# A graph layer on one core: the joined result turned by 32x32 blocks on VectorE, with stores and loads of 128-byte runs

## The chip, the cores and the metric

One Trainium2 chip, one of its cores. The metric is the device time of one execution in microseconds (us). Engines are named as in the profile: PE is TensorE (PEld its weight loads), DVE is VectorE, ACT is ScalarE, POOL is GpSimd, SP is SyncE; SPq is SP's own queue, from which the transfers are issued.

## The reference, cut to what matters

```python
# x (16, 512, 128), adj (16, 512, 512), W (7, 144, 128), W_edges (7, 16), b (512, 128), all float32
h = maximum(layernorm(x), 0)
A = [adj, adj, shifted, adj.T, adj.T, shifted.T, eye]          # seven relations
HW[r] = h @ W[r, :128] + (W_edges[r] @ W[r, 128:])              # a constant row per relation
out = x + max over r of (A[r] @ HW[r]) + b
```

`shifted` is a rolled identity. The kernel treats relations 2, 5 and 6 (its `EYE`) without an adjacency, 0 and 1 (`FWD`) with adj, 3 and 4 (`BWD`) with its transpose. The kernel forms adj @ h and adj.T @ h once each and multiplies them by W afterwards.

## The kernel before, in words

Sixteen batches are worked one after the other, two to a turn of the loop (`k` is the pair, `q` the half, b = 2k + q); nearly all tiles are doubled (`x_sb`, `a_sb`, `best`, `o_sb` ..., one for each q). Every engine has its own hand-written order of work, and semaphores tie them together. I call "step b" what `step(k, q, left)` (L297, L412, L580, L816) issues.

Everything is computed feature by node: a 128x512 tile has the features on the partitions and the 512 nodes of a batch along the row. Every float32 product is made of three passes (L720) over high and low parts (`a_hi`/`a_lo`, `h_hi`/`h_lo` and so on).

In step b TensorE does, in this order: `fwd` of the batch (four chunks of three passes), between them the relations of `EYE` and the two `FWD` relations of the batch before (`along`, L774); then it turns the first half of the next batch's adjacency (`turn_a`, L678) and its h (`turn_h`, L692); then `bwd` with the `BWD` relations of the batch before; then the second half of the next adjacency; and last `turn_best` (L712): four transposes of 128x128, which bring the finished maximum of the batch before (`best`, feature by node) to node by feature in the PSUM bank `turn_ps`.

VectorE keeps the running maximum (`join`, L534) and makes low parts; at the start of step b its `finish` (L545) adds the turned maximum from `turn_ps` and `xb_sb` (x plus bias) into `o_sb`. ScalarE makes the high parts, and `fill` (L381) writes row sums of the adjacency, times a constant, into the PSUM banks in which `along` then adds. GpSimd makes the low parts of the adjacency (`split_a`, L264) and of h (`split_h`, L271), the reciprocal deviation, and `xb_sb` (`add_bias`, L279), which reads the same `x_sb` as the layer norm.

SP issues every transfer. In step b (L211): store of batch b-2 when `out_ready` says so (L209, one transfer, runs of 512 bytes); x of batch b+2 (L177), which waits for `h_ready` and `xb_ready`; the adjacency of batch b+2 (L180) in four transfers of 256 KB, each when its piece of `a_lo` is made; then `spread_sums` (L196): the row sums (8x128) go to DRAM (L201), SP waits for them to be stored (L202), and one transfer copies them to all 128 partitions (`sum_all`, L203, 512 KB written). In step 0 `spread_sums` stands first. All these transfers stand in one queue and use the same 16 DMA engines.

After step 15 there is a tail: the last relations, the last `turn_best(k, 0)` (batch 14), and for batch 15 two halves of 256 columns: join (L666), transposes (L880), add (L673) and two stores on SP (L246).

Of the kernel before, what the change touches and what calls it, by code (L numbers as in the profile page):

```python
# [6 lines left out]
def gnn_layer(nc, x, adj, W, W_edges, bias, out):  # L7

# [25 lines left out]
    S = 2 * C  # L34
    PAIRS = B // 2
# [3 lines left out]
    with ctx:  # L39
# [22 lines left out]
        bias_sb = sb("bias_sb", [P, C, O])  # L62
# [8 lines left out]
        xb_sb = pair(sb, "xb_sb", [P, C, F])  # L71
# [21 lines left out]
        o_sb = pair(sb, "o_sb", [P, C, O])  # L93
# [9 lines left out]
        def at_bank(b, i):  # L103
# [6 lines left out]
        x_loaded = pair(sem, "x_loaded")  # L110
# [29 lines left out]
        half_filled, half_done, half_joined, half_turned, half_out_ready = (  # L140
            sem(s) for s in ("half_filled", "half_done", "half_joined", "half_turned", "half_out_ready"))
# [29 lines left out]

        block = ctx.enter_context(nc.Block())

        @block.sync
        def _(sp):
            def load_x(k, q):
                sp.dma_start(x_sb[q][:], x[2 * k + q, :, :].rearrange("(j p) f -> p j f", p=P)).then_inc(x_loaded[q], 16)  # L177

            def load_a(k, q, j):
                sp.dma_start(a_sb[q][:, j, :], adj[2 * k + q, j * P:(j + 1) * P, :]).then_inc(a_loaded[q][j], 16)  # L180

            def reload_x(k, q):

                b = 2 * k + q
                sp.wait_ge(h_ready, b + 1)
                sp.wait_ge(xb_ready, b + 1)
                load_x(k + 1, q)

            def reload_a(k, q):
                b = 2 * k + q  # L190
                sp.wait_ge(a_turned[C - 1], b + 1)
                for j in range(C):
                    sp.wait_ge(a_lo_ready[j], b + 1)
                    load_a(k + 1, q, j)

            def spread_sums(k, q):  # L196
# [4 lines left out]
                sp.dma_start(sums_dram[q][:, :], sum_rows[q][:]).then_inc(sums_stored[q], 16)  # L201
                sp.wait_ge(sums_stored[q], 16 * (k + 1))  # L202
# [4 lines left out]
            def store(k, q):  # L207
                sp.wait_ge(out_ready, 2 * k + q + 1)
                sp.dma_start(out[2 * k + q, :, :].rearrange("(j p) o -> p j o", p=P), o_sb[q][:]).then_inc(out_stored[q], 16)  # L209

            def step(k, q, more, stored=True):  # L211

                if isinstance(k, int) and k == 0 and q == 0:
                    spread_sums(k, q)
                if stored:
                    store(k - 1, q)
# [3 lines left out]
                if not (isinstance(k, int) and k == 0 and q == 0):  # L220
# [14 lines left out]
            sp.dma_start(bias_sb[:], bias.rearrange("(j p) o -> p j o", p=P)).then_inc(bias_loaded, 16)  # L235
# [8 lines left out]
            for half, (ready, count) in enumerate(((half_out_ready, 1), (out_ready, B))):  # L244
                sp.wait_ge(ready, count)
                sp.dma_start(out[B - 1, half * HALF:(half + 1) * HALF, :].rearrange("(j p) o -> p j o", p=P),  # L246
                             o_sb[1][:, half * C // 2:(half + 1) * C // 2, :]).then_inc(out_stored[1], 16)
            sp.wait_ge(out_stored[0], 16 * PAIRS)
            sp.wait_ge(out_stored[1], 16 * (PAIRS + 1))

        @block.gpsimd
        def _(pool):
# [26 lines left out]
            def add_bias(k, q):  # L279
                b = 2 * k + q  # L280
                pool.wait_ge(x_loaded[q], 16 * (k + 1))
                wait(pool, out_ready, b - 1)
                pool.tensor_tensor(xb_sb[q][:], x_sb[q][:], bias_sb[:], ALU.add).then_inc(xb_ready, 1)  # L283

            def first_step():
# [7 lines left out]
                pool.wait_ge(bias_loaded, 16)  # L293
                add_bias(0, 0)
                add_bias(*ahead)

            def step(k, q, left):  # L297
                if is_batch(2 * k + q, 1):
# [4 lines left out]
                    split_a(k, q, 3)  # L303
                else:
# [22 lines left out]
            later_batches(pool, step)  # L327

        @block.scalar
        def _(act):  # L330
            def round_a(k, q, j):
                b = 2 * k + q
                act.wait_ge(a_loaded[q][j], 16 * (k + 1))
# [154 lines left out]
            fill(k, q, BWD[1], bwd_ps, filled[BWD[1]], slice(HALF, N))  # L488

        @block.vector  # L490
        def _(dve):
# [53 lines left out]
            def finish(k, q):  # L545
# [357 lines left out]
```

## Time and profile before

| what | us |
|---|---|
| device time of three executions | 229.6, 229.86, 560.38 |
| their median | 229.86 |
| the profiled execution's own device time | 230.07 |
| span of its trace | 228.3 |

The trace begins 0 us at its first instruction; what lies outside the span is 230.07 - 228.3 = 1.8 us. The granted TensorE clock is 0.998 of full over the run.

### The profile page before, as it was taken

How to read it: one execution, taken by the hardware profiler on the slowest of the kernel's cores; microseconds unless marked ns; L12 is line 12 of the kernel's file. 1: busy time of each engine (PE TensorE's matmuls, PEld its weight loads, DVE VectorE, ACT ScalarE, POOL GpSimd, SP SyncE). 2: the span in 40 equal slices, each digit the busy share in tenths (PEclk: the TensorE clock that was granted, in tenths of full speed). 3: DMA queues.
4: the chain of work that ended last, by engine and by line, in shares of the span. 5: the costliest groups of instructions: out<-in, count | busy, mean ns of one | idle time of the engine just before them, and what ended most of it. 6: DMA issues, size and time to landing. Idle time of an engine off the chain costs nothing.

```text
span 228.3 us, 4799 instructions
## 1 busy us (share of the span) xinstructions
PE 217.5 (95%) x1133; PEld 179.8 (79%) x1133; DVE 177.7 (78%) x387; ACT 186.1 (82%) x468; POOL 143.0 (63%) x163
## 2 busy tenths in 40 slices
PE   7888999999999999999999999999999999999981
PEld 5567677888888888888888888888888888888761
DVE  4896798787978878787878878787887879767473
ACT  3868998888988888897988889798888889886640
POOL 2491679578493948758493966949395784937200
PEclk9999999999999999999999999999999999999999
DMA  5948454726436372744537372653547265121203
GB/s 186 295 120 277 135 140 138 229 97 199 172 117 190 107 230 92 226 143 140 188 97 224 115 228 114 167 191 91 198 135 222 101 162 207 49 81 60 92 0 95
DMA packets 30385, 34.52 MB, mean 151 GB/s; under 512 B 2103, under 2 KB 20135, under 8 KB 30375
## 3 DMA queue, kind: packets, MB, share of 16 engines
q1 hardware_dynamic: 30375, 34.41, 47.4%
q8 instruction: 4, 0.07, 0.1%
q14 instruction: 6, 0.05, 0.1%
HBM read 30.14 MB, written 4.26 MB: 151 GB/s over the span
## 4 chain that ended last, share of the span: by engine, by line
PE 86%; DVE 5%; issue 2%; ACT 2%; DMA 2%; SPq 0%; DVEq 0%; ACTq 0%
PE at_ps L689 11%; PE rel_ps L721 11%; PE rel_ps L723 11%; PE rel_ps L722 11%; PE fwd_ps L721 6%; PE bwd_ps L721 6%; PE bwd_ps L723 6%; PE bwd_ps L722 6%; PE fwd_ps L723 6%; PE fwd_ps L722 6%; PE turn_ps L701 3%; PE turn_ps L717 3%; DMA a_sb<-in_adj 2%; DVE h_lo L635 1%; DVE best L540 1%
## 5 line engine op out<-in xcount | busy, mean ns | idle before, releaser
L268 POOL TENSOR_TENSOR a_lo<-a_sb,a_hi 128x512 fp32r<-128x512 f32 x62 | 79.2, 1301 | 53.5 <-ACT a_hi L336 53.5
L543 DVE TENSOR_TENSOR best<-rel_ps,best 128x512 f32<-128x512 f32 x62 | 42.4, 683 | 17.2 <-PE rel_ps L723 16.5
L514 DVE TENSOR_TENSOR at_lo<-at_ps,at_hi 128x512 fp32r<-128x512 f32 x62 | 41.1, 683 | 6.8 <-ACT at_hi L344 6.7
L384 ACT ACTIVATE rel_ps<-sum_all,c_col 128x512 f32<-128x512 f32 (+1 forms) x63 | 41.8, 679 | 3.8 <-DVE best L543 3.1
L336 ACT ACTIVATE a_hi<-a_sb 128x512 fp32r<-128x512 f32 x64 | 39.4, 616 | 3.5 <-DMA a_sb<-in_adj 3.5
L344 ACT ACTIVATE at_hi<-at_ps 128x512 fp32r<-128x512 f32 x62 | 36.3, 590 | 7.1 <-PE at_ps L689 7.1
L689 PEld LDWEIGHTS at_ps<-ident,a_sb 128*128 128x128 f32 x240 | 28.1, 141 | 4.1
L689 PE MATMUL at_ps<-ident,a_sb 128*128 128x128 f32 x240 | 31.2, 272 | 0.0
L540 DVE SCALAR_TENSOR_TENSOR best<-rel_ps,c_col,best 128x512 f32<-128x512 f32 x32 | 24.0, 750 | 5.7 <-PE rel_ps L723 4.5
L721 PE MATMUL fwd_ps<-at_hi,h_hi 128*128 128x512 f32 x64 | 26.8, 419 | 1.2 <-DVE at_lo L514 1.0
L721 PE MATMUL bwd_ps<-a_hi,h_hi 128*128 128x512 f32 x64 | 26.6, 415 | 0.3 <-POOL a_lo L268 0.3
L723 PE MATMUL fwd_ps<-at_hi,h_lo 128*128 128x512 f32 x64 | 25.2, 394 | 0.0
L723 PE MATMUL bwd_ps<-a_hi,h_lo 128*128 128x512 f32 x64 | 25.2, 393 | 0.0
L722 PE MATMUL fwd_ps<-at_lo,h_hi 128*128 128x512 f32 x64 | 25.0, 391 | 0.0
L722 PE MATMUL bwd_ps<-a_lo,h_hi 128*128 128x512 f32 x64 | 25.0, 390 | 0.0
L354 ACT ACTIVATE h_sb<-x_sb,shift,rstd 128x128 f32<-128x128 f32 x60 | 24.6, 483 | 0.0
L276 POOL TENSOR_TENSOR h_lo<-h_sb,h_hi 128x512 fp32r<-128x512 f32 x14 | 17.9, 1279 | 6.6 <-DVE h_hi L508 6.6
L283 POOL TENSOR_TENSOR xb_sb<-x_sb,bias_sb 128x512 f32<-128x512 f32 x16 | 21.0, 1318 | 1.4 <-DVE o_sb L550 1.4
L392 ACT ACTIVATE best<-rel_ps,c_col 128x512 f32<-128x512 f32 x16 | 11.0, 689 | 12.3 <-PE rel_ps L723 12.3
L721 PE MATMUL rel_ps<-ht_hi,w_hi 128*128 128x512 f32 x48 | 19.3, 401 | 1.4 <-issue 0.9
L722 PE MATMUL rel_ps<-ht_lo,w_hi 128*128 128x512 f32 x48 | 19.0, 395 | 0.0
L723 PE MATMUL rel_ps<-ht_hi,w_lo 128*128 128x512 f32 x48 | 18.9, 393 | 0.0
(104 smaller groups left out, 437.2 us busy)
## 6 DMA issues: line engine op xcount, KB each, us to landing
a_sb<-in_adj SPq DMA_DIRECT2D x64, 256.0 KB, 4.1
sum_all<-sums_dram SPq DMA_DIRECT2D x16, 512.0 KB, 3.6
x_sb<-in_x SPq DMA_DIRECT2D x16, 256.0 KB, 2.9
out<-o_sb SPq DMA_DIRECT2D x15, 256.0 KB, 2.3
w_sb<-in_L_gnn_W SPq DMA_DIRECT2D x1, 448.0 KB, 5.6
bias_sb<-in_L_gnn_b SPq DMA_DIRECT2D x1, 256.0 KB, 4.8
sums_dram<-sum_rows SPq DMA_DIRECT2D x16, 4.0 KB
out<-o_sb SPq DMA_DIRECT2D x2, 128.0 KB, 2.5
```

The lines of the kernel that those rows point to most:

```text
L268: pool.tensor_tensor(a_lo[q][:, j, :], a_sb[q][:, j, :], a_hi[q][:, j, :].bitcast(fp32), ALU.subtract).then_inc(a_lo_ready[j], 1)
L336: act.activation(a_hi[q][:, j, :], a_sb[q][:, j, :], ACT.Copy, accum_out=sums[q][:, 0, j:j + 1]).then_inc(a_hi_ready[j], 1)
L344: act.activation(at_hi[q][:, i, :], at_bank(b, i)[:], ACT.Copy, accum_out=sums[q][:, 1, i:i + 1]).then_inc(at_hi_ready[i], 1)
L354: last = act.activation(h_sb[q][:, j, :], x_sb[q][:, j, :], ACT.Relu, bias=shift[q][:, j:j + 1], scale=rstd[q][:, j:j + 1])
L384: act.activation(to[:, cols], sum_all[q][:, 0 if r in FWD else 1, cols], ACT.Copy, scale=c_col[:, r:r + 1]).then_inc(after_it, 1)
L514: dve.tensor_tensor(at_lo[q][:, i, :], at_bank(b, i)[:], at_hi[q][:, i, :].bitcast(fp32), ALU.subtract).then_inc(at_lo_ready[i], 1)
L540: dve.scalar_tensor_tensor(out=best[q][:], in0=held[:], scalar=c_col[:, r:r + 1], in1=best[q][:], op0=ALU.add, op1=ALU.max).then_inc(joine ...
L543: dve.tensor_tensor(best[q][:], held[:], best[q][:], ALU.max).then_inc(joined[r], 1)
L689: last = pe.transpose(at_bank(b, i)[:, j * P:(j + 1) * P], a_sb[q][:, j, i * P:(i + 1) * P], ident[:])
L721: pe.matmul(out, w_hi_, m_hi, start=start, stop=False, skip_group_check=onto)
L722: pe.matmul(out, w_hi_, m_lo, start=False, stop=False, skip_group_check=onto)
L723: return pe.matmul(out, w_lo_, m_hi, start=False, stop=stop, skip_group_check=onto)
```

## The change

- The turned result no longer passes through TensorE and `turn_ps`. VectorE turns `best` by blocks of 32x32 (`dve.transpose`, at the end of its step, after `split_fwd`) into a new tile pair `turned`. In it partition 32g + n, column 32c + f holds feature 32g + f of node 32c + n.
- GpSimd, not VectorE, adds `turned` and `xb_sb` into `o_sb` (`finish`), after the second `split_a` pair of its step; `add_bias` moves behind it and is made for the batch before.
- x is loaded a second time in this block layout (`xp_sb`, one buffer, four transfers of 32 partitions, 512 runs of 128 bytes each), and so is the bias; the output is stored in it by four such transfers. These loads of x stand between the store of the sums and the wait for it.
- SP's order in a step: x of b+2 (waits for `h_ready` alone), the adjacency of b+2 as one transfer of 1 MB after all four pieces of `a_lo`, the store of b-2, the sums, x by blocks, `sum_all`.
- In the tail each half is joined, turned and added by VectorE; its stores are issued half from SP, half from ScalarE.

```diff
@@ SP
+            def store_by_blocks(nodes, held, stored):
+                for g in range(G):
+                    sp.dma_start(by_blocks(nodes)[g],
+                                 held[g * Q:(g + 1) * Q, :].rearrange("n (c f) -> n c f", f=Q)).then_inc(stored, 16)
             def reload_x(k, q):
-                sp.wait_ge(h_ready, b + 1)
-                sp.wait_ge(xb_ready, b + 1)
+                sp.wait_ge(h_ready, 2 * k + q + 1)
                 load_x(k + 1, q)
+            def load_xp(k, q):
+                wait(sp, xb_ready, 2 * k + q)
+                load_by_blocks(xp_sb, x[2 * k + q, :, :], xp_loaded)
             def reload_a(k, q):
                 sp.wait_ge(a_turned[C - 1], b + 1)
                 for j in range(C):
                     sp.wait_ge(a_lo_ready[j], b + 1)
-                    load_a(k + 1, q, j)
+                sp.dma_start(a_sb[q][:], adj[2 * k + 2 + q, :, :].rearrange("(j p) m -> p j m", p=P)
+                             ).then_inc(a_loaded[q][C - 1], 16)
             def spread_sums(k, q):
                 sp.dma_start(sums_dram[q][:, :], sum_rows[q][:]).then_inc(sums_stored[q], 16)
+                if is_batch(b, 0):
+                    load_by_blocks(bias_sb, bias, bias_loaded)
+                else:
+                    load_xp(k, q)
                 sp.wait_ge(sums_stored[q], 16 * (k + 1))
             def step(k, q, more, stored=True):
-                if stored:
-                    store(k - 1, q)
                 if more:
                     reload_x(k, q)
                     reload_a(k, q)
+                if stored:
+                    store(k - 1, q)
+                if first:
+                    load_xp(k, q)
+                else:
                     spread_sums(k, q)
@@ GpSimd
             def add_bias(k, q):
-                pool.wait_ge(x_loaded[q], 16 * (k + 1))
+                pool.wait_ge(xp_loaded, G * 16 * (b + 1))
                 wait(pool, out_ready, b - 1)
-                pool.tensor_tensor(xb_sb[q][:], x_sb[q][:], bias_sb[:], ALU.add).then_inc(xb_ready, 1)
+                pool.tensor_tensor(xb_sb[q][:], xp_sb[:], bias_sb[:], ALU.add).then_inc(xb_ready, 1)
+            def finish(k, q):
+                pool.wait_ge(best_turned, b + 1)
+                pool.wait_ge(xb_ready, b + 1)
+                wait(pool, out_stored[q], G * 16 * k)
+                pool.tensor_tensor(o_sb[q][:], turned[q][:], xb_sb[q][:], ALU.add).then_inc(out_ready, 1)
             def step(k, q, left):
-                    add_bias(k, q)
                     split_a(k, q, 2)
                     split_a(k, q, 3)
+                    finish(k - 1, q)
+                add_bias(*before(k, q))
@@ VectorE
-            def finish(k, q):
-                dve.tensor_tensor(o_sb[q][:].rearrange("p j o -> p (j o)"), turn_ps[:],
-                                  xb_sb[q][:].rearrange("p j o -> p (j o)"), ALU.add).then_inc(out_ready, 1)
+            def turn_best(k, q):
+                dve.wait_ge(joined[ORDER[-1]], b + 1)
+                wait(dve, out_ready, b - 1)
+                dve.transpose(turned[q][:], best[q][:]).then_inc(best_turned, 1)
             def step(k, q, left):
-                    finish(k - 1, q)
                 split_fwd(k, q)
+                turn_best(*prev)
@@ VectorE, tail
+                dve.wait_ge(joined_, count)
+                dve.transpose(turned[q][:, cols], best[q][:, cols]).then_inc(half_turned, 1)
+                dve.wait_ge(half_turned, half + 1)
+                dve.tensor_tensor(o_sb[q][:, cols], turned[q][:, cols], xb_sb[q][:, cols],
+                                  ALU.add).then_inc(half_out_ready, 1)
@@ TensorE
             def step(k, q, left):
                     turn_a(*ahead, 3)
-                    turn_best(*prev, b + 2)
@@ TensorE, tail
-            turn_best(k, 0, B)
-                    last = pe.transpose(at_ps[half][:, j * P:(j + 1) * P], best[q][:, j * P:(j + 1) * P], ident[:])
```

`by_blocks(nodes)` is `nodes.rearrange("(c n) (g f) -> g n c f", n=32, f=32)`. `turn_h` on TensorE also loses its wait for `out_ready`, as `turn_ps` now holds h alone; ScalarE and TensorE wait for one semaphore of a reloaded adjacency instead of four.

## Rows read from the trace of the kernel before

**Rows 1.** The page's first part: busy time, share, instructions, by engine.
```profile
PE 217.5 (95%) x1133; PEld 179.8 (79%) x1133; DVE 177.7 (78%) x387; ACT 186.1 (82%) x468; POOL 143.0 (63%) x163
```

**Rows 2.** Stretches: length; PE, PEld, DVE, ACT, POOL busy; clock, DMA share, GB/s.
```profile
36.66:49.80 13.14, 13.14 (x71) 11.08 (x71) 10.59 (x23) 11.50 (x31) 9.30 (x12) 1.00 0.53 172
...
115.50:128.64 13.14, 13.14 (x73) 11.06 (x72) 10.60 (x23) 11.52 (x31) 9.13 (x11) 1.00 0.50 160
```

**Rows 3.** The chain that ended last, at 115 us: start, us, what.
```profile
115.31 0.44 PE turn_ps L717 x4
115.74 0.23 PE fwd_ps L721
```

**Rows 4.** Groups of instructions by line.
```profile
L717 PE MATMUL turn_ps<-ident,best 128*128 128x128 f32 x60 | 9.0, 272 | 0.0
L508 DVE CAST h_hi<-h_sb 128x512 fp32r<-128x512 f32 x15 | 6.9, 458 | 1.9 <-ACT h_sb L354 1.8
```

**Rows 5.** VectorE in order of time, 114 to 118 us.
```profile
114.45 0.68 DVE L526 TENSOR_TENSOR fwd_lo<-fwd_ps,fwd_hi 128x512 fp32r<-128x512 f32 x1
115.88 0.69 DVE L550 TENSOR_TENSOR o_sb<-turn_ps,xb_sb 128x512 f32<-128x512 f32 x1 [0.74 <-PE turn_ps L717]
116.48 1.28 DVE L514 TENSOR_TENSOR at_lo<-at_ps,at_hi 128x512 fp32r<-128x512 f32 x2
```

**Rows 6.** GpSimd in order of time, 103 to 109 us.
```profile
103.75 1.31 POOL L283 TENSOR_TENSOR xb_sb<-x_sb,bias_sb 128x512 f32<-128x512 f32 x1
105.01 2.56 POOL L268 TENSOR_TENSOR a_lo<-a_sb,a_hi 128x512 fp32r<-128x512 f32 x2
108.17 1.28 POOL L276 TENSOR_TENSOR h_lo<-h_sb,h_hi 128x512 fp32r<-128x512 f32 x1 [0.60 <-DVE h_hi L508]
```

**Rows 7.** ScalarE and TensorE in order of time: the fill, its first reader.
```profile
104.61 1.29 ACT L384 ACTIVATE rel_ps<-sum_all,c_col 128x512 f32<-128x512 f32 x2
105.91 0.39 PE L721 MATMUL rel_ps<-fwd_hi,w_hi 128*128 128x512 f32 x1
117.17 0.69 ACT L392 ACTIVATE best<-rel_ps,c_col 128x512 f32<-128x512 f32 x1 [0.86 <-PE rel_ps L723]
```

**Rows 8.** SP's queue in order of time, 96 to 113 us.
```profile
96.77 0.30 SPq L201 DMA_DIRECT2D sums_dram<-sum_rows  x1
...
109.91 0.30 SPq L201 DMA_DIRECT2D sums_dram<-sum_rows  x1
112.28 0.35 SPq L203 DMA_DIRECT2D sum_all<-sums_dram  x1
```

**Rows 9.** Stretches with one kind of transfer, columns as in rows 2.
```profile
12.60:14.00 1.40, 1.21 (x5) 1.05 (x6) 1.40 (x4) 0.99 (x2) 1.32 (x3) 1.00 0.68 168
196.20:197.40 1.20, 1.20 (x7) 0.98 (x6) 0.93 (x2) 1.20 (x3) 1.20 (x2) 1.00 0.75 219
106.00:112.00 6.00, 6.00 (x35) 5.05 (x34) 4.44 (x11) 5.24 (x14) 2.85 (x3) 1.00 0.72 219
111.00:112.00 1.00, 1.00 (x6) 0.78 (x5) 0.99 (x2) 1.00 (x4) 0.00 (x0) 1.00 0.15 54
204.00:206.00 2.00, 2.00 (x10) 1.66 (x9) 1.80 (x4) 2.00 (x8) 1.28 (x2) 1.00 0.68 262
```

**Rows 10.** The page's last part: transfers, KB each, median us to landing.
```profile
sum_all<-sums_dram SPq DMA_DIRECT2D x16, 512.0 KB, 3.6
```

**Rows 11.** Step 1 and 2: SP's queue, GpSimd, ScalarE in order of time.
```profile
31.98 0.33 SPq L201 DMA_DIRECT2D sums_dram<-sum_rows  x1
27.62 3.97 POOL L268 TENSOR_TENSOR a_lo<-a_sb,a_hi 128x512 fp32r<-128x512 f32 x3
38.90 1.30 ACT L384 ACTIVATE rel_ps<-sum_all,c_col 128x512 f32<-128x512 f32 x2
```

**Rows 12.** The tail: VectorE and SP's queue in order of time.
```profile
224.29 0.76 DVE L673 TENSOR_TENSOR o_sb<-at_ps,xb_sb 128x256 f32<-128x256 f32 x2 [0.36 <-PE at_ps L880]
224.75 1.61 SPq L246 DMA_DIRECT2D out<-o_sb  x2
```

More of the change, by code:

```diff
@@ L170, in later_batches, with by_blocks, store_half @@
             step(PAIRS - 1, 1, 0)
+        def by_blocks(nodes):
+            return nodes.rearrange("(c n) (g f) -> g n c f", n=Q, f=Q)
+        def store_half(queue, half, blocks):
+            cols = slice(half * HALF, (half + 1) * HALF)
+            queue.wait_ge(half_out_ready, half + 1)
+            for g in blocks:
+                queue.dma_start(by_blocks(out[B - 1, cols, :])[g],
+                                o_sb[1][g * Q:(g + 1) * Q, cols].rearrange("n (c f) -> n c f", f=Q)
+                                ).then_inc(half_stored, 16)
         block = ctx.enter_context(nc.Block())
@@ L219, in step @@
                     reload_a(k, q)
-                if not (isinstance(k, int) and k == 0 and q == 0):
+                if stored:
+                    store(k - 1, q)
+                if first:
+                    load_xp(k, q)
+                else:
                     spread_sums(k, q)
@@ L243, in _ @@
             store(PAIRS - 1, 0)
[L244 to L249, printed above, removed]
+            for half in range(2):
+                store_half(sp, half, range(0, G // 2))
+            sp.wait_ge(out_stored[0], G * 16 * PAIRS)
+            sp.wait_ge(out_stored[1], G * 16 * (PAIRS - 1))
+            sp.wait_ge(half_stored, 2 * G * 16)
         @block.gpsimd
@@ L327, in _ @@
             later_batches(pool, step)
+            add_bias(PAIRS - 1, 1)
+            finish(PAIRS - 1, 0)
         @block.scalar
@@ L332, in round_a @@
                 b = 2 * k + q
-                act.wait_ge(a_loaded[q][j], 16 * (k + 1))
+                act.wait_ge(a_loaded[q][C - 1 if not (isinstance(k, int) and k == 0) else j], 16 * (k + 1))
                 wait(act, bwd_done, b - 1)
@@ L488, in _ @@
             fill(k, q, BWD[1], bwd_ps, filled[BWD[1]], slice(HALF, N))
+            for half in range(2):
+                store_half(act, half, range(G // 2, G))
         @block.vector
@@ L657, in _ @@
             join(k, q, FWD[0])
-            finish(k, 0)
             join(k, q, FWD[1])
@@ L680, in turn_a @@
                 if i == 0:
-                    for j in range(C):
+                    for j in range(C) if isinstance(k, int) and k == 0 else (C - 1,):
                         pe.wait_ge(a_loaded[q][j], 16 * (k + 1))
@@ L694, in turn_h @@
                 pe.wait_ge(h_ready, b + 1)
-                if isinstance(b, int) and b == 1:
-                    pe.wait_ge(ht_lo_ready, 1)
-                else:
-                    wait(pe, out_ready, b - 2)
-                    wait(pe, ht_lo_ready, b)
+                wait(pe, ht_lo_ready, b)
                 for j in range(C):
@@ L710, in turn_sums @@
                 pe.transpose(to[0:S, 0:P], sums[q][:].rearrange("p t c -> p (t c)"), ident[:]).then_inc(sums_turned, 1)
-            def turn_best(k, q, ht_count):
-                b = 2 * k + q
-                pe.wait_ge(joined[ORDER[-1]], b + 1)
-                pe.wait_ge(ht_lo_ready, ht_count)
-                for j in range(C):
-                    last = pe.transpose(turn_ps[:, j * P:(j + 1) * P], best[q][:, j * P:(j + 1) * P], ident[:])
-                last.then_inc(best_turned, 1)
             def passes(out, w_hi_, w_lo_, m_hi, m_lo, start, stop, onto=False):
```

49 lines of the change are left out of this document (20 added, 29 removed).

## The prediction

> **What bounds the kernel now.** I read the page's busy times first: TensorE is busy 95% of the span, the next engine (ScalarE) 82% [rows 1]. A share over the whole is no proof, so I cut the run at each start of a batch's first forward pass. Twelve stretches in a row, from 36.66 us on, are each 13.14 us long (within 0.02 where the cut was exact); the two shown hold 13.14 us of TensorE work, 10.6 of VectorE, 11.5 of ScalarE and 9.1 to 9.3 of GpSimd, at full granted clock, with the DMA engines busy for half of the time [rows 2]. So in steady state TensorE never waits, and a step costs what TensorE issues in it. The chain of waits says the same from the other side: it runs through TensorE alone, and the four transposes of `best` are a link of it worth 0.44 us [rows 3] (the 272 ns of one transpose in the group are its full length, pipelined with its neighbours, so the chain's figure counts, not 4 x 272) [rows 4]. The start (to 36.66) and the tail behind step 15 lie outside this, and I take them apart below.
>
> **The change part by part.** I write t for the time from a step's first forward pass, which stands at 102.35 in the stretch that I read.
>
> *TensorE loses turn_best.* 60 transposes are 15 batches [rows 4]; 14 of them lie in steps 1 to 14 and one in the tail. 14 x 0.44 us [rows 3] = -6.1 us, if the step then lasts 12.70 us and nobody else is late.
>
> *VectorE.* It loses the add from `turn_ps` (0.69 us, after 0.74 us of waiting) and gains a turn by blocks of 128x512. No row shows one. Nearest rows: 458 ns for the copy of that size from SBUF to SBUF [rows 4], 0.69 for an add [rows 5]; I take 0.69, as the dearer is the safer, and keep both. Its place is free: `split_fwd` ends at 114.45 + 0.68 = 115.13, and the next instruction after the old add started at 116.48 [rows 5], 1.35 us later. Up to there the turn costs nothing; VectorE even comes 0.6 us earlier to `at_lo`. The Trainium skill (VectorE: DVE Perf Modes, The three transpose paths) gives 311 ns for a bfloat16 128x128 turn on VectorE; four of these would be an estimate of 1.24 us, still inside the gap. No row here shows it.
>
> *GpSimd.* It gains one add of 1.3 us per step (as `xb_sb`, 1.31 [rows 6]): 9.1 + 1.3 = 10.4 of 12.70. In order: both `a_lo` pieces come 1.3 us earlier, since `add_bias` went behind them (done at 106.3, not 107.57), then finish to 107.6, bias add to 108.9, `h_lo` to 110.2 instead of 109.45. `h_lo` is needed only by the next step's first forward pass (115.7 [rows 3]), and the idle time left in a step, 12.70 - 10.4 = 2.3 us, lies right behind it, since GpSimd then waits for ScalarE's next high parts. Cost nothing.
>
> *The transfers.* Price of a packet, from stretches in which one kind moves, as share x length x 16 engines over packets: a store of 256 KB is 512 packets of 512 bytes, 0.75 x 1.2 us / 32 per engine = 28 ns. One x load and four adjacency loads took 0.72 x 6.0 = 4.3 us; less 0.9 for x, 3.4 us for 1 MB, or 106 ns per 2 KB. `sum_all`: 0.68 x 2 = 1.36 us [rows 9]. A packet of 128 bytes is in no row. In proportion to bytes it would be 7 ns; at the price of its 512-byte neighbour 28. In the stretch 12.60 to 14.00 the 112 packets of 4 bytes of `wedge` go by beside 512-byte ones: 0.68 x 1.4 x 16 = 15.2 engine-us, less (168 GB/s x 1.4 us / 512 =) 459 x 28 ns = 12.9, leaves 2.3, at most 21 ns for each [rows 9]. I take 15 ns, between 7 and 21, and keep 28 for both directions and 56 for a write as the far end. Per step the change adds 2048 such packets of x and replaces the 512 of the store by 2048: 128 per engine each way. DMA time per step: 0.50 x 13.14 [rows 2] = 6.6, less 0.9, plus 256 x 15 ns = 3.8: 9.5 of 12.70 us. Not a bound by its sum, but by its order.
>
> The Trainium skill (DMA: Bandwidth & Descriptors, Specifications) wants at least 512 bytes for line rate and says that below this the engine reads, modifies and writes: it speaks against this change; twice the 28 ns, worked out in the third rival, is what it would cost here. The same page (Why small descriptors are slow) counts 32 bytes per cycle and some 3 cycles on top: 7 cycles against 19, an estimate of 10 ns by our 28, by which there would be room. The second alone agrees with the at most 21 ns of the 4-byte packets.
>
> *Order of the queue.* The sums are the transfer with a deadline. They were issued at 96.77 and the fill that needs them began at 104.61, 7.84 us later [rows 7, 8]; TensorE reads the first fill at 105.91, 0.6 us after its end (104.61 + 0.69) [rows 7]. With a step of 12.70 us the limit from issue to landing is 7.84 - 0.44 + 0.6 = 8.0 us. Call the issue S (t = 7.56, at 109.91). Ahead of it in the queue now lie the adjacency, issued at 106.3 when the last `a_lo` is done, moving from 107.2 to 110.6, and the store of batch b-2 (ready at 107.6, so behind it): all of this ends at S + 0.7 + 128 w, w the price of a written packet. The sums were reported stored 1.1 us after the data ahead of them had gone (the stretch 111 to 112 has a share of 0.15, so they ended at about 111.15 [rows 9]; the wait ended at 112.28 [rows 8]), and `sum_all` lands 3.6 us after its issue [rows 8, 10]. Landing: S + 5.4 + 128 w, so w may be up to 20 ns. The x by blocks is issued before `sum_all`: S + 0.7 + 128 (w + r) + 1.36 + 1.2 must stay below S + 8.0, so w + r may be up to 37 ns. At 15 ns each both hold (7.3 and 7.1). Seven more issues on SP and three fewer of the adjacency make 12 a step, at 0.30 to 0.35 us [rows 8] some 4.2 us of 12.70; they make nobody wait: out_ready comes at t = 5.3, xb_ready at 6.6, both before S.
>
> *Moves that cost nothing:* the adjacency lands by t = 9, and TensorE turns it a step later, under other work; x is issued earlier than before; the bias, now behind the first sums, delays a `sum_all` whose first fill comes only in step 1, when ScalarE has rounded most of the next adjacency.
>
> *Once, at the start.* In step 1 the last `a_lo` is done at 27.62 + 3.97 = 31.6, the sums follow at 31.98 [rows 11]. Until now only the last 256 KB stood ahead of them; now it is the whole 1 MB, to 32.5 + 3.4 = 35.9. Stored 37.0, landing 40.6; the fill of step 2 wanted it at 38.90 - 0.44 + 0.6 = 39.1 [rows 11]. A single transfer may move faster, in 2.7 us at the rate of `sum_all` (1.36 us for 512 KB [rows 9]); so 0.8 to 1.5, and I take +1.0.
>
> *Tail.* VectorE does joins, two turns and two adds in a row. It loses 0.69 us (the add of batch 14, as [rows 5]), gains that batch's turn, and its last add ends as before (about 225.05 = 224.29 + 0.76 [rows 12]), counted without the 6.1. Two short stores on each of two queues replace one that took most of 1.61 us; 64 small packets per engine behind the last add cost 1.0 instead of 0.5. I take +0.1 (-0.5 to +2).
>
> Sum against the profiled execution: 230.07 - 6.1 + 1.0 + 0.1 = 225.1 us. Its own time is 0.2 above the median of the three (229.86), less than the sum resolves, so I leave it: 225.1 us, 2.1% below the median.
>
> **The rivals.**
> 1. *As forecast*, 223 to 226.5 us; the low end is a start that costs nothing.
> 2. *Most of it given back, within 2%.* The small packets cost somewhat more than 18.5 ns each, or the start and tail more than 1.1 us. A lateness e in S + ... shows as a stall of e/2 per step, as the stall lies ahead of S and moves S, but not the adjacency and the store. At w + r = 42: e = 0.64, 0.32 x 13 steps = +4.2: 229.3 us. For it: the margin is under 1 us on a 12.7 us step. Against: the 4-byte packets.
> 3. *Slower: the queue of small packets becomes the bound.* Place: `sum_all` behind store and x. At 28 ns each, e = 0.7 + 7.2 + 2.56 - 8.0 = 2.4, stall 1.2 per step, +15.6: 240.7 us. If a write is paid twice (56), DMA alone needs 6.6 - 0.9 + 10.8 = 16.5 us per step, 3.8 over 12.70: +49, 274 us. It turns slower by 2% from w + r = 48 ns (stall 0.72 x 13 = 9.4). For it: 28 ns is the nearest measured size, and nothing shows a write of under 512 bytes.
> 4. *Another engine takes TensorE's place*, so that the step stays near 13.1. ScalarE has 11.5 of 12.70 and still waits 0.86 us for TensorE at its `join_first` [rows 7]; 0.44 less leaves 0.4. Time 229 to 231, in the "within 2%" case. Little speaks for it.
>
> **How the numbers follow.** The forecast's own range, 223 to 226.5 us, gets 0.50; the 2% edge (0.98 x 229.86 = 225.3) lies in it, and the short end is the longer one, so 0.42 of it is faster by over 2% and 0.08 within. Rivals 2 and 4 get 0.22 together, rival 3 0.28. So: faster 0.42, same 0.30, slower 0.28. The 2% is about what a measurement of this kernel can tell from no change. Range 222.8 to 238: up to a stall of 1.0 per step (225.1 + 13); beyond it lies half of rival 3, below it nearly nothing.
>
> **What would show it.** Right: stretches of 12.70 us with TensorE at 12.7; no transposes of `best` in the chain; packets of 128 bytes below 18 ns; SP waits for stored sums under 3.5 us; one stall of about 1 us at the first fill of step 2. Wrong: idle time of the fill (L384 before) ended by the `sum_all` transfer in every step, DMA share near 1, or steps still of 13.1 us with another engine named ahead of TensorE.

## The result, and the profile after

| kernel | device us, all executions | median | ratio to before, 95% interval |
|---|---|---|---|
| before | 229.55, 229.6, 229.86, 560.38 | 229.73 | 1 |
| changed | 233.18, 233.69, 235.24, 238.22 | 234.47 | 1.020 [1.015, 1.024] |
| changed, measured again (`e0_after`) | 235.32, 236.62, 238.43, 239.16 | 237.52 | 1.035 [1.029, 1.041] |

The change costs 2 to 3.5% where I had forecast a gain of 2%. The ratios are of fast executions, each against the kernel before as it was measured beside it; 560.38, 238.22 and 239.16 us are slow ones. The changed kernel also scatters more: its eight executions span 6 us, where the 48 of before that were measured beside the experiments lie between 228.0 and 230.7. Its profiled execution is the 238.22 us one, which also fell to half clock for some us at step 2; where a reading must not depend on that, I read the profile of `e0_after` (235.32 us, span 233.5), whose clock fell only in the tail.

The page of the changed kernel, first part (columns as in rows 1), the group that matters, and two of the transfers (KB each, median us from issue to landing):

```profile
PE 217.8 (92%) x1069; PEld 173.9 (74%) x1069; DVE 179.2 (76%) x389; ACT 185.8 (79%) x468; POOL 161.7 (68%) x178
...
L433 ACT ACTIVATE rel_ps<-sum_all,c_col 128x512 f32<-128x512 f32 (+1 forms) x63 | 41.6, 676 | 16.6 <-DMA sum_all<-sums_dram 14.2
...
sum_all<-sums_dram SPq DMA_DIRECT2D x16, 512.0 KB, 4.5
...
out<-o_sb SPq DMA_DIRECT2D x60, 64.0 KB, 4.2
```

The 60 matmuls of `turn_best` and the 4 of the tail's transposes are gone (1133 to 1069 [rows 1]), yet TensorE's busy time is 0.3 us longer, part of it at half clock, and the span 8.1. `sum_all` now lands 4.5 us after its issue, not 3.6 [rows 10], and ScalarE's fill spends 14.2 us of idle time on it, of which before shows nothing among its waits.

I cut the run again, here from one start of a step's second `turn_a` group (L739, eight transposes; L689 before) to the next. In us:

```
before    13.62, then 13.14 to 13.15 twelve times
changed   17.93 13.85 12.99 13.36 13.03 13.88 12.99 13.97 12.99 13.57 13.05 13.22 13.24
e0_after  15.86 13.00 13.63 12.99 13.38 13.46 13.34 13.74 12.99 13.21 13.23 13.06 12.99
```

Two things stand in these rows. Even the best steps last 12.99 us, not 12.70. And most of the others are up to 1 us longer than that. The sum over `e0_after`: twelve steady steps together 159.0 us against 157.7 before (+1.3, forecast -5.3), the step at the first fill +2.2 (forecast -0.4 + 1.0), all the rest, tail and the step behind the cuts among it, +1.7 (forecast -0.4 + 0.1). Together +5.2 us, the difference of the two profiled executions.

### The profile page after: what moved, and what is told of

The parts are those of the page before. It is cut to its first block, busy times and chain, and to the rows that moved or that the text cites. A ratio compares the mean times of both kernels' runs of the same rounds, so it can differ in the third digit from the quotient of the medians.

```text
span 236.4 us, 4833 instructions
## 1 busy us (share of the span) xinstructions
PE 217.8 (92%) x1069; PEld 173.9 (74%) x1069; DVE 179.2 (76%) x389; ACT 185.8 (79%) x468; POOL 161.7 (68%) x178
## 4 chain that ended last, share of the span: by engine, by line
POOL 50%; issue 31%; DVE 5%; DMA 4%; PE 3%; SPq 2%; POOLq 1%; ACT 1%; ACTq 0%; DVEq 0%
POOL a_lo L308 20%; POOL h_lo L316 8%; POOL o_sb L330 7%; POOL xb_sb L323 7%; POOL rstd L300 6%; DMA a_sb<-in_adj 2%; DMA sum_all<-sums_dram 2%; POOL var_eps L297 1%; DVE h_lo L685 1%; POOL neg_mean L298 1%; DVE best L594 1%; POOLq L154 1%; SPq L207 1%; SPq L202 1%; DVE stats L546 1%
## 5 line engine op out<-in xcount | busy, mean ns | idle before, releaser
L433 ACT ACTIVATE rel_ps<-sum_all,c_col 128x512 f32<-128x512 f32 (+1 forms) x63 | 41.6, 676 | 16.6 <-DMA sum_all<-sums_dram 14.2
L739 PEld LDWEIGHTS at_ps<-ident,a_sb 128*128 128x128 f32 x240 | 28.8, 143 | 4.3 <-issue 0.2
L739 PE MATMUL at_ps<-ident,a_sb 128*128 128x128 f32 x240 | 31.9, 276 | 0.0
L761 PE MATMUL fwd_ps<-at_hi,h_lo 128*128 128x512 f32 x64 | 25.5, 398 | 0.0
L323 POOL TENSOR_TENSOR xb_sb<-xp_sb,bias_sb 128x512 f32<-128x512 f32 x16 | 20.9, 1308 | 4.8 <-DMA xp_sb<-in_x 4.8
L330 POOL TENSOR_TENSOR o_sb<-turned,xb_sb 128x512 f32<-128x512 f32 x15 | 19.3, 1287 | 1.5 <-DVE turned L601 1.5
L759 PE MATMUL rel_ps<-fwd_hi,w_hi 128*128 128x512 f32 x32 | 14.0, 438 | 6.5 <-ACT rel_ps L433 6.3
```

The costliest lines, as they stand in the source:

```text
L323: pool.tensor_tensor(xb_sb[q][:], xp_sb[:], bias_sb[:], ALU.add).then_inc(xb_ready, 1)
L433: act.activation(to[:, cols], sum_all[q][:, 0 if r in FWD else 1, cols], ACT.Copy, scale=c_col[:, r:r + 1]).then_inc(after_it, 1)
L739: last = pe.transpose(at_bank(b, i)[:, j * P:(j + 1) * P], a_sb[q][:, j, i * P:(i + 1) * P], ident[:])
L759: pe.matmul(out, w_hi_, m_hi, start=start, stop=False, skip_group_check=onto)
L761: return pe.matmul(out, w_lo_, m_hi, start=False, stop=stop, skip_group_check=onto)
```

## Three places, read in the trace

**The steps that are never 12.70.** The changed kernel around the end of a step, in order of time (start, us, engine, line, operation, idle before):

```profile
133.02 1.04 PE L739 MATMUL at_ps<-ident,a_sb 128*128 128x128 f32 x8
...
133.20 0.68 DVE L577 TENSOR_TENSOR fwd_lo<-fwd_ps,fwd_hi 128x512 fp32r<-128x512 f32 x1
...
133.80 0.70 DVE L601 STREAM_TRANSPOSE turned<-best 128x512 f32<-128x512 f32 x1
134.06 0.19 PEld L759 LDWEIGHTS fwd_ps<-at_hi,h_hi 128*128 128x128 f32 x1 [0.24 <-issue]
```

TensorE's next pass loads its weights at 134.06, 0.24 us after it could and 0.18 us after `fwd_lo` ended (133.20 + 0.68 = 133.88). Before, `fwd_lo` ended at 115.13 [rows 5] and the next pass began at 115.74 [rows 3]: the four transposes of `best` covered it. The trace names only "issue" for this wait; that it is `fwd_lo` is a hypothesis here, and e3 and e4 test it. The turn itself takes 0.70 us on VectorE.

**The steps that are late.** `e0_after`: GpSimd, SP's queue and ScalarE, each in order of time:

```profile
106.06 2.55 POOL L308 TENSOR_TENSOR a_lo<-a_sb,a_hi 128x512 fp32r<-128x512 f32 x2
108.57 1.30 POOL L330 TENSOR_TENSOR o_sb<-turned,xb_sb 128x512 f32<-128x512 f32 x1
...
108.85 0.38 SPq L228 DMA_DIRECT2D a_sb<-in_adj  x1
110.03 2.70 SPq L207 DMA_DIRECT2D out<-o_sb  x4
112.78 1.16 SPq L236 DMA_DIRECT2D sums_dram<-sum_rows  x1
114.13 1.94 SPq L202 DMA_DIRECT2D xp_sb<-in_x  x4
116.11 0.49 SPq L242 DMA_DIRECT2D sum_all<-sums_dram  x1
...
112.26 0.27 ACT L428 ACTIVATE sum_rows<-rel_ps 8x128 f32<-8x128 f32 x1 [0.30 <-PE rel_ps L756]
...
121.03 1.30 ACT L433 ACTIVATE rel_ps<-sum_all,c_col 128x512 f32<-128x512 f32 x2 [0.70 <-DMA sum_all<-sums_dram]
```

The store could be issued only when GpSimd's add was done, at 108.57 + 1.30 = 109.87. The sums are ready at 112.53. SP is still issuing the store (four issues in 2.70 us, where I had 0.30 to 0.35 us for each); the sums' own issue lasts 1.16 us against 0.30 [rows 8]; then come four issues of x by blocks; `sum_all` leaves at 116.11 and has landed at 121.03, after 4.9 us and not 3.6. From sums ready to landing 8.5 us, over the limit of 8.0. By `e0_after`'s waits this befalls the fill in 12 places and goes on to TensorE (engine, line, releaser: us in all, times, longest; the first line is SP's own wait for the stored sums):

```profile
SPq L242 <- DMA sums_dram<-sum_rows: 2.8, 2, 2.6
...
ACT rel_ps L433 <- DMA sum_all<-sums_dram: 13.1, 12, 4.0
PEld rel_ps L759 <- ACT rel_ps L433: 9.7, 11, 2.4
PEld fwd_ps L759 <- issue: 5.4, 15, 1.4
```

SP waits for the stored sums in 2 places of 16 only (before: in all 16, 25.5 us). In the others it comes to that wait so late that they are long stored: `sum_all` leaves when SP has finished its issues, and the path that ended last ran through SP's issuing.

**The tail.** `e0_after`'s chain that ended last (start, us, what), from step 15's queue on SP to the last relations:

```profile
213.10 1.26 POOL o_sb L330
...
214.37 0.33 SPq L207
...
216.38 0.40 SPq L236
...
216.82 0.32 SPq L202
...
218.78 3.98 DMA sum_all<-sums_dram
...
222.84 0.70 ACT rel_ps L433
...
224.09 0.24 PE rel_ps L760
...
226.30 0.43 PE fwd_ps L760
```

The last row sums were made at 213.01 to 213.28, but SP stands at the store of batch 13, which since the change is released by GpSimd behind its `a_lo` pieces (214.36). Sums, x, `sum_all` follow one after the other, and the fill of the last relations idles 4.04 us, TensorE 1.89. (The page's chain puts 51% of the span on GpSimd, as it passes here from the store to GpSimd's add. That GpSimd, busy 69%, is not the bound is shown by e2 below: its chain lies on TensorE with 80%.) Two windows behind it (columns as in rows 2):

```profile
225.00:227.00 2.00, 2.00 (x6) 1.21 (x5) 1.68 (x3) 1.03 (x3) 0.00 (x0) 0.50 0.66 103
227.00:229.00 2.00, 1.37 (x7) 1.14 (x5) 1.70 (x4) 0.00 (x0) 0.00 (x0) 0.71 0.17 28
```

After this idle stretch the granted clock falls to 0.50 (1.2 of 2.4 GHz) and a pass of 512 columns takes 0.43 us where it took 0.24. From the start of the last row sums to the end of the span `e0_after` needs 233.5 - 213.01 = 20.5 us, before 228.3 - 209.97 = 18.3: +2.2, which is the +1.7 and more. (e9 below has before's tail unchanged and needs 17.0 by the span, and by device time 19.7 where before needs 20.1; so this difference is known to some tenths.) The profiled execution of the changed kernel shows the same behind its stall in step 2, 2.37 us of idle TensorE; its step lasts 17.93 us, that of `e0_after`, whose TensorE idled 1.96 us there and kept its clock, 15.86 us. TensorE after that stall, and the windows behind it:

```profile
42.84 0.50 PE L759 MATMUL rel_ps<-fwd_hi,w_hi 128*128 128x512 f32 x1 [2.37 <-ACT rel_ps L433]
```

```profile
44.00:46.00 2.00, 2.00 (x7) 1.41 (x6) 0.96 (x2) 1.55 (x4) 0.49 (x1) 0.50 1.07 369
46.00:48.00 2.00, 2.00 (x15) 1.98 (x13) 0.89 (x2) 0.69 (x2) 0.79 (x1) 0.68 0.71 114
```

## The experiments

My theory after the result: two causes, (A) `fwd_lo` uncovered, worth 0.27 us in every step, and (B) `sum_all` late, because of what stands ahead of it. For B the rivals are the price of small packets (my rival 3), the order alone, and the transfer of 1 MB. The ratios are to the kernel before as measured beside each run: medians of 229.71 us for e0 to e3, 229.52 for e4 to e7, and 229.47, on another chip, for e8 to e10.

| run | edit to the changed kernel | median | ratio [95%] | steps: second, then |
|---|---|---|---|---|
| e1 | runs of 512 bytes | 229.36 | 0.997 [0.995, 1.000] | 15.51, 12.97 to 13.0 |
| e2 | sums first in the queue | 229.53 | 0.999 [0.997, 1.001] | 15.23, 12.97 to 13.03 |
| e3 | `fwd_lo` ahead of one join | 236.67 | 1.028 [1.024, 1.031] | 18.08, 12.72 to 13.9 |
| e4 | e2 and e3 | 224.97 | 0.979 [0.975, 0.983] | 15.27, 12.72 |
| e5 | reload in four pieces | 230.99 | 1.006 [1.002, 1.009] | 14.14, 14.54, then 12.96 to 13.0 |
| e6 | e4, and sums first in step 1 too | 223.22 | 0.972 [0.969, 0.975] | 13.01, 12.70 to 12.72 |
| e7 | e6 with runs of 512 bytes | 223.15 | 0.972 [0.968, 0.976] | 12.98, 12.70 to 12.72 |
| e8 | sums first in step 15 alone | 235.29 | 1.024 [1.016, 1.031] | 17.64, 12.99 to 13.45 |
| e9 | kernel before, `fwd_lo` ahead of one join | 228.79 | 0.997 [0.995, 1.000] | 13.14, 13.14 to 13.15 |
| e10 | e6 with the reload in four pieces | 223.46 | 0.976 [0.971, 0.980] | 12.97, 12.70 to 12.72 |

("Second" is the step at the first fill; before has 13.62 there.)

### e0_after: the changed kernel once more

> The changed kernel as it is, once more, for a profile without the dips of the granted clock. Theory A (two causes in a step: the row sums wait in SP's queue behind small packets, and TensorE's first forward pass now waits 0.2 us for the low part of the forward product that VectorE makes last but one; plus once 2 to 3 us in step 2 and some 4 us in the tail, all behind the sums) expects about 233.5 us, the shortest steps at 13.0 us and never at 12.70, and idle time of the fill ended by the transfer of the sums. Rival B (the dips of the clock in the profile of after are the loss) expects 228 to 229 us when the clock does not dip.

It is told above: slower again, with the same two patterns. Rival B is out: at full clock outside the tail it is no faster.

### e1_runs512: the same transfers in runs of 512 bytes

```diff
-                for g in range(G):
-                    sp.dma_start(by_blocks(nodes)[g],
-                                 held[g * Q:(g + 1) * Q, :]...).then_inc(stored, 16)
+                sp.dma_start(nodes.rearrange("(j p) f -> p j f", p=P),
+                             held[:].rearrange("p (j f) -> p j f", f=F)).then_inc(stored, 16)
```

The same for x and the bias (one transfer each). What it computes is not the layer: x is added in another layout, and the stores of all but the last batch put blocks in the wrong places.

> The changed kernel with every transfer of x by blocks, of the bias and of the output made as one transfer with runs of 512 bytes (so the output lies in wrong places and x is added in the wrong layout; the bytes moved are the same). Theory A: the small packets and their four issues of 0.5 us each are most of what delays the sums, but the order in the queue stays: 512 packets instead of 2048 take 0.9 us instead of 2.1, so the landing comes 2.4 us earlier: no stall in the steady steps, 13.0 us each, but still a stall of about 1 us in step 2 and the tail's wait for the store of batch 13. About 229 us. Rival C (the order alone costs, whatever the packets) expects 232 us or more. Rival D (the small packets are all of it and steps then last 12.70 us) expects 225 us.

The late steps are gone; the fill waits for `sum_all` in two places, 4.9 us in all, at the start and in the tail. The steps are 12.97 to 13.0 and not 12.70, so A stands apart from the packets. But e1 takes away six issues a step on SP as well as small packets, and it is SP that comes free: it now waits for the stored sums every time.

```profile
SPq L240 <- DMA sums_dram<-sum_rows: 31.6, 16, 3.9
```

### e2_sums_first: only the order

```diff
 # schedule of a step on SP: x, adjacency, then
-                if stored:
-                    store(k - 1, q)
-                if first:
-                    load_xp(k, q)
-                else:
-                    spread_sums(k, q)
+                if not first:
+                    spread_sums(k, q)
+                if stored:
+                    store(k - 1, q)
+                load_xp(k, q)
```

and in `spread_sums` the bias or x by blocks no longer stands between the sums and `sum_all`.

> The changed kernel with SP's order changed and nothing else: after the adjacency come the sums, the wait for them and the copy to all partitions, then the store of batch b-2, then x by blocks (packets of 128 bytes as before). Theory A: all steady steps at 13.0 us (0.15 us below the 13.14 of the kernel before, not 12.70, because TensorE still waits for the low part of the forward product), no wait of the fill except once in step 2 (about 1.5 us, the 1 MB in front), tail as in the kernel before: 230 - 2.1 + 1.5 = about 229 us. Rival E (128-byte packets slow the DMA engines for everything else, wherever they stand in the queue) expects steps of 13.3 us and more, 232 us or over.

The packets are all there, the late steps are not. Two of the waits of e2, and one of its steps (columns as in rows 2):

```profile
ACT rel_ps L430 <- DMA sum_all<-sums_dram: 1.9, 1, 1.9
...
PEld fwd_ps L756 <- issue: 4.9, 15, 0.9
```

```profile
109.17:122.14 12.97, 12.94 (x67) 10.68 (x66) 11.56 (x24) 11.52 (x30) 10.23 (x12) 1.00 0.68 180
```

The one wait left is in the step at the first fill; the tail has none and is as long as before (18.3 us from the last row sums on). The wait of `fwd_ps` for "issue" is untouched, 15 times. So B is made by what stands ahead of `sum_all`, and it costs 5 to 8 us (234.47 or 237.52, less 229.53).

### e3_fwd_lo_first: only A

```diff
-                join(k, q, EYE[2])
                 split_fwd(k, q)
+                join(k, q, EYE[2])
                 turn_best(*prev)
```

> The changed kernel with two VectorE instructions of each step exchanged: the low part of the forward product is made before the join of the last eye relation, not behind it. Theory A: the 0.2 to 0.25 us of idle time before the first forward pass goes, shortest steps 12.70 us; but the sums still land when they do, so where the fill waits the gain goes into its wait. Between 0 and 2 us faster than the changed kernel: 232 to 233.5 us. A rival that the 0.2 us is TensorE's own cost of starting a new group behind transposes expects no step under 12.95 us.

The shortest step is 12.72 us, as A wants it, and of the 15 waits of `fwd_ps` for "issue" 2 are left (1.7 us). But the time hardly follows: 236.67 us is 0.85 below `e0_after`, within the scatter and outside the 232 to 233.5 that I expected. The waits for `sum_all` grow from 13.1 to 18.4 us.

```profile
ACT rel_ps L433 <- DMA sum_all<-sums_dram: 18.4, 13, 4.5
```

A shorter step asks for `sum_all` earlier; as long as B is there, it takes most of what A gives: twelve steady steps are together 158.8 us, against 159.0 in `e0_after`. The step at the first fill (18.08 for 15.86 us) is longer because TensorE idled 3.17 us there and fell to half clock.

### e4_both: A and B cured together

The edits of e2 and e3.

> The order of e2 (sums before the store and x by blocks) and the exchange of e3 (low part of the forward product first) together. Theory A: with the sums out of the way the exchange now pays: steady steps of 12.70 us, 13 x 0.28 = 3.6 us less than e2_sums_first, and 0.4 at the start: 225.5 us. If the 0.28 us were TensorE's own cost of starting behind transposes: 229.5 us, steps of 12.98.

Two of its waits:

```profile
ACT rel_ps L430 <- DMA sum_all<-sums_dram: 2.6, 1, 2.6
...
PEld fwd_ps L756 <- issue: 1.6, 2, 1.4
```

Steps of 12.72 us throughout, and the wait at the end of each step is gone (15 to 2): that settles `fwd_lo` as what the trace called "issue". 224.97 us is 0.1 us from my forecast, but in a kernel with two more edits. The one wait for `sum_all` left makes the first-fill step 15.27 us.

### e5_reload4: the adjacency in four transfers of 256 KB again

```diff
                 for j in range(C):
                     sp.wait_ge(a_lo_ready[j], b + 1)
-                sp.dma_start(a_sb[q][:], adj[2 * k + 2 + q, :, :]...)
+                    load_a(k + 1, q, j)
```

> The changed kernel with the adjacency reloaded in four transfers of 256 KB again, each when its piece is done; nothing else. Theory A: the pieces for j = 0 to 2 leave before the last low part is ready, so the store of batch b-2 and the sums come up to 1 us earlier behind them: stalls of the fill shrink from 0.5 us a step on average to about 0.1, and step 2 to 1.5: between 231 and 234 us where the changed kernel runs at 233 to 237. Rival F (three more issues on SP cost as much as the earlier start gives) expects no difference from the changed kernel.

SP's queue in a step of e5, in order of time:

```profile
102.91 4.49 SPq L212 DMA_DIRECT2D a_sb<-in_adj  x4
108.33 1.99 SPq L207 DMA_DIRECT2D out<-o_sb  x4
110.37 0.40 SPq L235 DMA_DIRECT2D sums_dram<-sum_rows  x1
...
112.93 0.49 SPq L241 DMA_DIRECT2D sum_all<-sums_dram  x1
```

The pieces leave as their `a_lo` come, from 102.91 on, so the data is moved earlier; the store lands 2.1 us after its issue instead of 4.2, the four store issues take 1.99 us instead of 2.70, the sums' issue 0.40 instead of 1.16, and the late steps in steady state are gone (steps 12.96 to 13.0). The start is still late (14.14 and 14.54), and so is the tail, whose wait of 3.8 us is the longest of the four that remain:

```profile
ACT rel_ps L432 <- DMA sum_all<-sums_dram: 6.8, 4, 3.8
```

So three things together make the late steps: the whole megabyte just ahead, the transfers in runs of 128 bytes, and the order. To take away any one ends them in steady state; none is the cause alone. Two questions stay open. Whether the 128-byte transfers count by their packets or by their four issues each, no run tells, as e1 takes both away; the number of issues alone it is not, as e5 makes three more a step. And no run moves GpSimd's add, which releases the store, to an earlier place.

### e6_all_three: the sums ahead in step 1 as well

```diff
                 if more:
                     reload_x(k, q)
+                if is_batch(2 * k + q, 1):
+                    spread_sums(k, q)
+                if more:
                     reload_a(k, q)
-                if not first:
+                if not first and not is_batch(2 * k + q, 1):
                     spread_sums(k, q)
```

on top of e4.

> As e4_both, and in step 1 alone the sums go ahead of the 1 MB reload too. Theory A: the once-only wait of the fill in step 2 (1.9 us in e2_sums_first) goes as well: 224 us, 2.5% below the kernel before. If that wait has another cause it stays and the time is that of e4_both.

The best kernel of all, 223.22 us, 2.8% below the kernel before and 5 to 6% below the changed one (223.22 against 234.47 or 237.52). One of its steps (columns as in rows 2), SP's queue in it, and the wait that was 5.4 us in 15 places:

```profile
105.31:118.02 12.71, 12.71 (x68) 10.64 (x67) 10.79 (x24) 11.53 (x30) 10.52 (x13) 1.00 0.69 186
```

```profile
107.22 0.30 SPq L236 DMA_DIRECT2D sums_dram<-sum_rows  x1
109.24 0.35 SPq L238 DMA_DIRECT2D sum_all<-sums_dram  x1
109.86 2.15 SPq L207 DMA_DIRECT2D out<-o_sb  x4
112.19 2.56 SPq L202 DMA_DIRECT2D xp_sb<-in_x  x4
```

```profile
PEld fwd_ps L759 <- issue: 0.3, 1, 0.3
```

TensorE is busy through the whole step, `sum_all` leaves 2.0 us after the sums, and nothing waits for it anywhere. The start costs nothing (13.01 us at the first fill, down from 15.27). The other twelve steps are together 12 x 0.43 = 5.2 us shorter than before (forecast 12 x 0.44).

### e7_all_three_512 and e10_all_three_reload4: does what is left still cost?

e7 is e6 with the edit of e1 (and puts the output in wrong places as e1 does); e10 is e6 with the edit of e5.

> As e6_all_three, with x by blocks, bias and all stores but the last batch's made with runs of 512 bytes, one transfer each (output in wrong places, x added in the wrong layout). Theory A: the small packets cost nothing where nobody waits behind them: the same time as e6_all_three within 0.5 us. Rival E (they take something from the other transfers wherever they stand) expects it 1 us or more faster than e6_all_three.

> e6_all_three with the adjacency reloaded in four transfers again. Theory A: with the sums ahead of the small packets there is room for the 1 MB transfer, so the pieces bring nothing: 223 us within 0.5, steps of 12.70 us. If the single transfer cost something of its own (and not only by what waits behind it), this would be 1 us or more faster.

223.15 and 223.46 beside 223.22: with the deadline met, neither four issues in place of one, nor the 4096 packets of 128 bytes per step, nor the single megabyte costs anything that can be measured. This is the other half of e1, e2 and e5.

### e8_last_step_order: the tail alone

In step 15 only, `spread_sums` before the store:

```diff
+                last = is_batch(2 * k + q, B - 1)
+                if last:
+                    spread_sums(k, q)
                 if stored:
                     store(k - 1, q)
...
-                else:
+                elif not last:
                     spread_sums(k, q)
```

> The changed kernel with one step's order on SP exchanged: in step 15 alone the sums and x by blocks go ahead of the store of batch 13. Theory A: the fill behind step 15 no longer waits (3.8 to 4.5 us of idle time ended by the transfer of the sums in the tail), the steady steps stay as uneven as before: 2.5 to 4 us below the changed kernel, so 230 to 234 us by how much the steady steps stall in the run. If the tail's wait were covered by the last joins anyway: no difference.

SP's queue in the tail of e8:

```profile
214.63 0.28 SPq L236 DMA_DIRECT2D sums_dram<-sum_rows  x1
216.81 1.91 SPq L202 DMA_DIRECT2D xp_sb<-in_x  x4
218.76 0.49 SPq L242 DMA_DIRECT2D sum_all<-sums_dram  x1
```

A miss: the wait shrinks only from 4.0 to 3.1 us. The sums leave at once (they were made at 214.34 to 214.61), but the x by blocks inside `spread_sums` still stands ahead of `sum_all`, and waits for the x add of batch 14 on GpSimd, which ends at 216.78. From the last row sums on the run needs 233.5 - 214.34 = 19.2 us, between before's 18.3 and `e0_after`'s 20.5. In the device times (233.4 to 237.0 us in four executions) this gain of 1.3 us can't be told. So the store was one part of the late tail, and the x by blocks the other: e2, which moves both, has 18.3.

### e9_before_fwd_lo_first: the exchange in the kernel before

> The kernel before with nothing changed but the exchange of e3 (the low part of the forward product ahead of the last eye join). Theory A: there the four transposes of the joined result stand between, TensorE never waited for it, so steps stay at 13.14 us and only the first forward pass of step 2 may start 0.3 to 0.7 us earlier: 229.2 to 229.7 us. If it came out at 226 or less, the gain of e4 and e6 would not be one that the change brought with it.

228.79 us; all steps are 13.14, and only the step at the first fill gets shorter (13.62 to 13.14). In steady state the exchange is worth nothing while the transposes cover `fwd_lo`, and 0.27 us a step once they are gone (e4 against e2). With the exchange on both sides the change, cured, is worth 5.6 us (228.79 - 223.22, measured on two chips), 2.4%.

## Why the prediction was wrong, by its own steps

Three steps failed. "Nobody else is late" did not hold: `fwd_lo` was, which took 3.5 us of the saving in twelve steps. The landing of `sum_all`, with issues of which "they make nobody wait" was said, came after its limit: 3.1 us in twelve steps and 1.7 at the start. The tail was put at +0.1 us and took the rest, 2.0. One by one, with what was right:

- *TensorE's saving, -6.1 us by "12.70 us and nobody else is late".* The size of the removed work was right (12.70 to 12.72 in e4 and e6). The condition was wrong: `fwd_lo`, which I had in [rows 5] with its end at 115.13 and used only to place the turn, had its wait hidden by the transposes that went. Measured 12.99: 0.15 us per step, so 14 x 0.15 = 2.1 in place of 6.1. I had asked of ScalarE what would be late next (rival 4), and not of VectorE.
- *VectorE's turn, 0.69 us.* Measured 0.70, and its place behind `fwd_lo` was free. By the Trainium skill's figure (VectorE: DVE Perf Modes, The three transpose paths) my estimate had been 1.24 us; the runs decide for 0.70, for float32 of 128x512.
- *GpSimd, +1.3 us a step at no cost.* In steady state the busy time was right (10.2 to 10.6 us, o_sb 1.30; forecast 10.4). But I let the sum of its work speak and not its order: a store now waits for GpSimd's `finish`, and in step 15 this holds the sums' queue. That is the missed term of the tail.
- *Packets of 128 bytes, 15 ns.* Right. Two stretches of the changed kernel with one kind of transfer, writes first, then x by blocks:

```profile
229.50:230.00 0.50, 0.50 (x5) 0.46 (x4) 0.50 (x1) 0.00 (x0) 0.00 (x0) 1.00 0.77 119
222.50:223.00 0.50, 0.50 (x4) 0.41 (x3) 0.03 (x1) 0.00 (x0) 0.00 (x0) 1.00 0.73 117
```

  0.77 x 0.5 us x 16 engines over 119 GB/s x 0.5 us / 128 bytes (465 packets) is 13 ns; for reads 0.73 and 117 give the same. Read and write together 26 ns, under the 37 and the 48 of my bounds. The Trainium skill (DMA: Bandwidth & Descriptors, Specifications) speaks of reading, modifying and writing below 512 bytes: in busy time no such price shows here, a write costs what a read does. Its count under Why small descriptors are slow, by which my estimate was 10 ns, is the nearer one.
- *Order of the queue, landing at S + 7.3.* Here the sign was lost. The time of `sum_all`'s issue agrees (3.6 us after the sums were ready, forecast 0.7 + 1.9 + 1.1 = 3.7), but by luck: I had added up data moving ahead and the wait for the stored sums, and in the trace it is SP's issues, 0.25 us of the store's, 1.16 of the sums', 1.94 of x by blocks and 0.2 between them. Then I added the 3.6 us of a quiet queue. Behind x by blocks and beside a store still moving it took 4.9 us, and 4.3 to 4.5 in the median; e6, where nothing small stands ahead, has 3.9. I had two estimates, one by the wait and one by the queue, and took the larger; they add, in part. The margin was 0.7 us, this term alone +1.3.
- *Twelve issues at 0.30 to 0.35 us, "they make nobody wait".* Wrong, and with the landing above it is the step at which B was lost. I had counted an issue's own 0.35 us and nothing up to the next: four of x by blocks take 1.94 us, one every 0.53. Behind the megabyte the four of the store take 2.70 us, and the sums' issue 1.16 (median over `e0_after` 1.37, forecast 0.30). SP was still issuing when the sums were ready, and made `sum_all` wait in 14 of 16 places.
- *Rival 2's rule of e/2 per step.* With 8.5 against 8.0, e/2 is 0.25 us; the twelve steps of `e0_after` average 13.25, 0.26 over the shortest. The agreement in size is not a test of the mechanism, and the alternation of late and early steps I did not foresee and have not explained.
- *Rival 3* named the right place (`sum_all` behind store and x) with the wrong reason (28 or 56 ns a packet).
- *Start, +1.0 us.* The place was right and the size not: before already had 0.5 us there (13.62), and the fill idled 2.6 us in `e0_after` and 2.99 in the changed kernel's profile. That the order in step 1 is its cause is shown by e6 against e4.
- *Tail, +0.1 us.* Measured +2.2. Missed were the wait for `sum_all` and the half clock after it. In e2, which has neither, the tail is as long as before, and the forecast holds; the small stores at its end cost little.

The account against the forecast, by the profile of `e0_after`: 225.1 + 6.6 (twelve steps, 159.0 - 12 x 12.70) + 1.7 (the step at the first fill, +2.24 for +0.56) + 2.0 (the rest, +1.7 for -0.3) = 235.4, and it took 235.3. Of the 6.6, 12 x 0.29 = 3.5 is `fwd_lo` and 3.1 the late sums.

## What to carry to other kernels

Before work is taken from the engine that bounds, list every wait that stands right behind it and read how much of each it covers; here 0.44 us of transposes hid 0.29 us of wait for another engine. A transfer with a deadline goes first in its queue: adding large or many-run transfers ahead of it costs through issue time and landing time, although the engines' share stays at 0.7; so time a queue by its issues too, from the start of one to the start of the next. And cure such waits together: the exchange alone showed next to nothing (e3), the order alone only brought back the time of before (e2), and both with the start gave the forecast gain.

## What the runs showed of the hardware that I had not expected

- A packet of 128 bytes takes 13 ns of an engine, written or read, against 28 ns for one of 512 bytes [rows 9]: four times the packets cost about twice the time.
- The issue of a transfer on SP is not of fixed length: 0.30 us for the sums in the step of e6 above, 1.16 us behind a megabyte and 2048 small packets in that of `e0_after`, whose sixteen lie between 0.29 and 1.85 us.
- The landing time of one and the same 512-KB transfer goes from 3.6 us (before) over 3.9 (e6), 4.0 (e2) and 4.2 (e1, e7) to 4.3 and 4.5 (the changed kernel), all medians, and 4.9 in the step read above. What stands ahead is part of it; e7, with runs of 512 bytes, is no quicker than e6.
- After stalls of TensorE of 2.4 us (step 2 of the changed kernel's profile) and of about 2 us (tail of `e0_after`) the granted clock stood at 0.50 for the next 2 us or more, and the stalls were paid twice. `e0_after` idled 1.96 us in step 2 and kept its full clock there. In that step e3 (3.17 us idle) and e8 (2.20) fell too, and e1 (1.60), e2 (1.30) and e4 (1.98) did not; but in the tail of e3, 2.38 us of idle time were followed by full clock. So the length of the stall alone doesn't decide it, and what else does these runs don't show. With the half clock, and stalls 0.2 to 1.2 us longer, the step at the first fill took 17.93, 18.08 and 17.64 us, without it 15.86; so it costs more than the stall alone, and is at least one source of the scatter of the changed kernel.
